# Four-layer GNN stack: the last layer runs its score products ahead of the attended product of two pairs before, and the value product ahead of the new pair's first turn

## What is computed

```python
h = jnp.maximum(_layernorm(x, axis=-1), 0.0)
q = (h @ Wq + bq).reshape(b, n, H, HD); k = ...; v = ...
scores = jnp.einsum('bqhd,bkhd->bhqk', q, k) / jnp.sqrt(jnp.float32(HD))
scores = scores + (1.0 - adj)[None, None, :, :] * -1000000000.0
attn = jax.nn.softmax(scores, axis=-1)
out = jnp.einsum('bhqk,bkhd->bqhd', attn, v).reshape(b, n, d)
x = x + out @ Wo + bo
```

## Time and profile before

| | us |
|---|---|
| median of 3 runs (715.76 to 717.35) | 716.94 |
| the profiled execution, whole | 716.58 |
| its span, first to last instruction | 714.8 |
| PE busy in the span | 692.3 (97%) |
| DVE busy | 627.9 (88%) |
| ACT busy | 555.9 (78%) |
| POOL busy | 462.1 (65%) |

### The profile page before, as it was taken

One profiled execution on the slowest core, in us unless ns is written; L12 is line 12 of the kernel. 1 busy time (PEld: TensorE's weight loads), 2 busy tenths in 40 slices (PEclk: granted clock), 3 DMA queues, 4 the chain that ended last, 5 costly groups with the idle time before them and its releaser, 6 DMA issues.

```text
span 714.8 us, 22548 instructions
## 1 busy us (share of the span) xinstructions
PE 692.3 (97%) x6938; PEld 652.9 (91%) x6938; DVE 627.9 (88%) x2618; ACT 555.9 (78%) x1892; POOL 462.1 (65%) x585
## 2 busy tenths in 40 slices
PE   5999999999999999999998999999999999999996
PEld 5999999999888888889997999999999999999994
DVE  5899888987799999699998999998889998899876
ACT  3665656565689999876665998889888988898895
POOL 2445454554587788588884776776677666766662
DMA  8222310000000000000000000000000000000001
GB/s 246 83 82 89 89 43 0 0 0 2 0 1 2 1 2 1 2 1 0 0 0 1 17 33 17 30 29 30 15 30 29 30 15 30 30 29 16 32 32 45
DMA packets 21710, 20.30 MB, mean 28 GB/s; under 512 B 2449, under 2 KB 21649, under 8 KB 21649
## 3 DMA queue, kind: packets, MB, share of 16 engines
q1 hardware_dynamic: 19456, 18.16, 8.0%
q10 hardware_dynamic: 2192, 1.44, 0.7%
HBM read 11.21 MB, written 8.39 MB: 27 GB/s over the span
## 4 chain that ended last, share of the span: by engine, by line
PE 89%; DVE 3%; ACT 3%; issue 2%; POOL 1%; DMA 1%; POOLq 0%; ACTq 0%; DVEq 0%
PE bank L397 43%; PE bank L1276 8%; PE bank L387 7%; PE bank L166 5%; PE bank L1262 5%; PE bank L1286 4%; PE bank L480 4%; PE bank L837 3%; PE bank L427 3%; PE bank L377 3%; PE bank L461 1%; PE bank L875 1%; PE bank L850 1%; ACT prob L1372 1%; DMA wk<-in_L_gnn_Wk_dram 1%
## 5 line engine op out<-in xcount | busy, mean ns | idle before, releaser
L1372 ACT ACTIVATE prob<-wide,small 128x128 f32<-128x128 f32 x504 | 195.5, 395 | 2.1 <-DVE small L1484 2.1
L1447 POOL TENSOR_TENSOR prob<-prob,small 128x512 f32<-128x512 f32 x127 | 132.3, 1043 | 100.1 <-DVE small L1498 98.1
L1484 DVE CUSTOM_DVE_ANT_0 wide<-bank,mbias 128x128 f32<-128x128 f32 x512 | 115.3, 286 | 0.1
L1372 ACT ACTIVATION_READ_ACCUMULATOR prob<-wide,small 128x1 f32 x504 | 97.2, 193 | 0.0
L155 POOL TENSOR_TENSOR rstd<-vare,mhalf 128x2 f32<-128x2 f32 x104 | 73.3, 704 | 20.5 <-DVE vare L144 20.2
L1276 PE MATMUL bank<-ident,prob 128*128 128x128 f32 x512 | 72.2, 273 | 3.8 <-POOL prob L1447 3.5
L636 POOL TENSOR_TENSOR rnorm<-norm,mhalf 128x2 f32<-128x2 f32 x32 | 22.3, 696 | 81.3 <-ACT relsq L577 81.3
L129 DVE BATCH_NORM_STATS2 stats<-xs 128x6 f32<-128x256 f32 (+1 forms) x176 | 65.6, 415 | 5.9 <-DMA xs<-in_x_dram 5.0
L239 POOL TENSOR_SCALAR xn<-xs,nmean,rstd 128x256 f32<-128x256 f32 x120 | 65.3, 554 | 5.5 <-POOL rstd L155 5.5
L1392 ACT COPY probT<-bank 128x512 f32<-128x512 f32 x96 | 52.3, 580 | 18.7 <-PE bank L1276 18.7
L1276 PEld LDWEIGHTS bank<-ident,prob 128*128 128x128 f32 x512 | 58.3, 140 | 5.5 <-POOL prob L1447 4.8
(11 more groups left out here) (168 smaller groups left out, 1933.1 us busy)
## 6 DMA issues: line engine op xcount, KB each, us to landing
out_dram<-xs SPq DMA_DIRECT2D x31, 256.0 KB, 2.1
xs<-in_x_dram SPq DMA_DIRECT2D x29, 256.0 KB, 2.7
xs<-in_x_dram ACTq DMA_DIRECT2D x1, 512.0 KB, 7.8
xs<-in_x_dram ACTq DMA_DIRECT2D x1, 256.0 KB, 4.3
wq<-in_L_gnn_Wq_dram SPq DMA_DIRECT2D x1, 256.0 KB, 3.9
wk<-in_L_gnn_Wk_dram ACTq DMA_DIRECT2D x1, 256.0 KB, 5.2
wv<-in_L_gnn_Wv_dram SPq DMA_DIRECT2D x1, 256.0 KB, 5.8
w<-in_L_gnn_W_dram SPq DMA_DIRECT2D x1, 256.0 KB, 7.4
```

The source lines that it names most:

```text
L1372: ins = nc.scalar.activation(prob[:, r, i, :], wide[:, r, i, :], ACT.Exp, bias=nmax[r][:, i:i + 1], scale=-1.0, accum_out=rsum[r][:, i:i + 1])
L1447: nc.gpsimd.tensor_tensor(prob[:, r, :, :], prob[:, r, :, :], rinv[r].unsqueeze(2).to_broadcast([128, QUAD, N]), ALU.mult).then_inc(prob_r ...
L1484: nc.vector.tensor_tensor_reduce(out=wide[:, r, i, :], in0=SS[r][:, i * N:(i + 1) * N], in1=mbias[:, :], scale=-1.0, scalar=3e38, op0=ALU. ...
```

## The change

Nothing is added or removed; all instructions and waits stay, and their places change. On TensorE `scores(p)` goes ahead of `attend(p-2)`, and `project_v(p+1)` goes ahead of `turn_prob(p,0)`. On ScalarE `copy_o(p-2)` goes behind `exponentials(p-1,3)`. On VectorE `low_o(p-2)` goes behind `mask_max(p,0)` and `inverse(p-1,3)`, and `inverse(p,2)` behind `copy_v`.

```diff
@@ TensorE, period
+                    scores(p)
                     if has(p, 2):
                         attend(p - 2, (v + 2) % 4)
-                    scores(p)
...
-                    turn_prob(p, 0)
                     if has(p, 0, LAST):
                         project_v(p + 1)
+                    turn_prob(p, 0)
@@ ScalarE, period
-                    if has(p, 2):
-                        copy_o(p - 2)
                     if has(p, 1):
                         exponentials(p - 1, 3)
+                    if has(p, 2):
+                        copy_o(p - 2)
                     exponentials(p, 0)
@@ VectorE, period
-                    if p > 1:
-                        low_o(p - 2)
                     mask_max(p, 0)
                     if p > 0:
                         inverse(p - 1, 3)
+                    if p > 1:
+                        low_o(p - 2)
...
                     copy_k(p + 1)
+                    copy_v(p + 1)
                     inverse(p, 2)
-                    copy_v(p + 1)
```

More of the change, by code:

```diff
@@ L1402, in period @@
                     relu_high(p + 1, TQ1 if isinstance(p, int) and p == 0 else TQ)
+                    if has(p, 1):
+                        exponentials(p - 1, 3)
                     if has(p, 2):
                         copy_o(p - 2)
-                    if has(p, 1):
-                        exponentials(p - 1, 3)
                     exponentials(p, 0)
```

## The result

The changed kernel takes 728.19 us (median of 4, 727.71 to 728.62) where the kernel before takes 716.35 in the same comparison (715.47 to 717.35): 11.8 us more, a ratio of 1.0165 with a 95% interval of 1.0147 to 1.0182. The forecast was 730.7 us, with 726.5 to 734.5 around it. The executions of one kernel come in two sets, with a mean granted clock of 1.000 and of 0.997 to 0.998, and the second takes 0.5 to 1.4 us longer; all four of the changed kernel are in the first, and in most of the experiments the median is taken over both.

A forecast was written before the change was run, and what follows sets the result against it. TensorE, 97% busy, was taken as the bound, its output product made to wait by the later `copy_o`: 29 x 0.50 = 14.5 us, less 0.35 at the start, on 716.58 gives 730.7 us, range 726.5 to 734.5.

The forecast's parts named there:

- What bounds the kernel: TensorE, 97% busy, almost never waits in the 29 full periods; the block whose input is ready latest decides.
- The chain: From the end of `turn_prob(p-1,1)` through ScalarE's copies and exponentials, `copy_o` and `low_o` to the output product, at 577.44.
- S: The moment at which TensorE takes up what follows `turn_prob(p-1,1)`; times in a period are counted from it.
- the other kind of period: Periods in which ScalarE starts 0.11 instead of 0.17 us behind S, so the output product's lateness is 0.36 us.
- The mean lateness: Output product on TensorE starts late by 0.42 or 0.36 us, 0.39 in the mean, in each of 29 periods.
- The longer block: Output product on TensorE, started on an emptied array, takes 1.53 instead of 1.42 us, 0.11 more a period.
- The value product on TensorE: Moving it ahead of `turn_prob(p,0)` costs 0 a period, with 0 to 0.09 us as bounds.
- Start and end: Waits of 1.03 and 0.23 us in periods 0 and 1 filled, together -0.35 us; last period 0.
- VectorE's late copies: `copy_v` may make the scores 0.1 or 0.2 us late, at no cost, since the output product waits 0.39 anyway.
- The rival of a second wait: VectorE's list makes the k product or scores late by 0.1 to 0.3 us a period: 734 to 739; chance 0.10.
- The rival of a saved drain: Transposes and scores on TensorE follow without the 0.20 us change of tiles, chain in time: 710.4 us; chance 0.03.
- The rival of GpSimd's lock on `low_o`: GpSimd's multiply `divide(p-1,3)` holds VectorE's `low_o` up, 20 us more: about 751 us; chance 0.04.

The follow-up runs named there:

- the runs with three, four and five exponentials: Changed kernel with `copy_o` behind three, four (the changed kernel itself) or five exponentials: 718.61, 728.19 and 740.30 us.
- The run with three: Changed kernel with `copy_o` behind three of the four exponentials and `low_o` between `mask_max(p,0)` and `inverse(p-1,3)`: 718.61 us, ratio 1.0032.
- the kernel with two: Changed kernel with `copy_o` behind two of the four exponentials and `low_o` between `mask_max(p,0)` and `inverse(p-1,3)`: 719.73 us, ratio 1.0041.

## Why the prediction was right

- **What bounds the kernel** held: the 29 full periods carried +12.95 of the change, and the block whose input is ready latest, the output product, is the one that waits.
- **The chain** held link by link, in S: the copy at 0.18 (0.17 was read from the rows of before), the first exponential at 1.15 (1.15), `copy_o` at 2.69 (2.70), `low_o` at 3.30 (3.33), its end at 3.99 (4.01), the output product at 4.04 (4.07). In the other kind of period the product comes at 403.04 - 399.07 = 3.97 (4.01). The mean lateness is 0.355 where 0.39 was summed; the runs with three, four and five exponentials show its slope.
- **The longer block** of a product that had to wait held: 1.53 for 1.42, taken from the block behind a change of tiles. The run with three adds that 0.10 is paid even with no wait in sight, when the weights come just in time.
- **The value product on TensorE** was taken at 0 with 0 to +0.09; it is -0.02, outside that bound.
- With these two the sum is 29 x (0.355 + 0.11 - 0.02) = 12.9 instead of 14.5, so 1.6 too high: 1.0 from the lateness and 0.6 from the value product.
- **Start and end**: -0.44 for -0.35, and -0.15 for 0. Of the two waits that were to be gone, the 0.23 is; the 1.03 came back as 0.99 one group later. With these 0.24 and the 0.46 of chance ahead of the first scores the whole is accounted for: the profiled executions differ by 11.9 where +14.15 was forecast.
- **VectorE's late copies**: said to be hidden, and shown so by the changed kernel with L144 moved. The scores were expected 0.1 or 0.2 late in such periods, under the longer wait; they are not late at all. The rival of a second wait did not come in the changed kernel; its mechanism is real, and came in the kernel with two, at 0.22 a time.
- **The rival of a saved drain** fell: with the scores straight behind the transposes they start at 590.63, and the last transposes' block 0.53 ahead, as the attended product's did (572.84 to 573.37). **The rival of GpSimd's lock on `low_o`** fell by the rows of `low_o` and of the multiply; that the multiply would lie over `low_o` was right. The Trainium skill (SBUF — State Buffer, Who interferes with whom) says that a VectorE instruction with two inputs in SBUF contends with a GpSimd instruction that reads SBUF, and that one with at most one does not. The trace agrees in both: L144, with two, is held, `low_o`, with one in PSUM, is not.

## What to carry to other kernels

When a producer and its consumer sit on different in-order engines, an operation moved behind others delays its consumer by the whole group that now stands ahead of it; add up the chain from the last common event (here the end of a group of transposes) and compare it with the time at which the consumer would start. An edit that moves a producer later on the busy engine may leave the other engines' lists nothing to repair: the attended product went 1.1 us later where the slack was 1.07 us, and with the best place of `copy_o` that was tried the weights still came just in time, not early. Parts of such a change are best timed apart: here one of them gained 0.1% and was hidden under the loss of the rest. And gains of a microsecond are best compared between executions at the same granted clock.

## What the runs showed of the hardware that was not expected

A product whose weights arrive just in time shows no wait in any view and is still 0.10 us longer over its 12 matmuls (1.52 against 1.42). And a VectorE operation of two columns, 0.15 us long, can last as long as a 1.04 us GpSimd multiply. In the changed kernel VectorE's and GpSimd's timelines have

```profile
587.72 0.39 DVE L143 SCALAR_TENSOR_TENSOR nmean<-mv 128x2 f32<-128x2 f32 x1
588.03 0.15 DVE L144 SCALAR_TENSOR_TENSOR vare<-mv 128x2 f32<-128x2 f32 x1
```

```profile
586.78 1.31 POOL L1442 TENSOR_TENSOR xs<-xs,rows 128x512 f32<-128x512 f32 x1
588.05 1.04 POOL L1447 TENSOR_TENSOR prob<-prob,small 128x512 f32<-128x512 f32 x1
```

where L144 is short; at 407.54 against 407.55, above, it is long. It was long in 5 to 18 of 29 periods in the kernels that kept its place, but for one with 1, and in none where it was moved to a place in which GpSimd was idle.

That the two start almost together is no accident. L143, just ahead of L144, takes 0.15 us where GpSimd is idle and 0.39 here, and it ends 14 to 26 ns behind GpSimd's bias (L1442; here both end at about 588.1), in all full periods of the kernels that kept its place. So it is held until the bias ends, and then L144 and the next multiply start within 25 ns of each other. Which of them comes first in the rows doesn't decide whether L144 is held: in the changed kernel it is long when it starts 23 ns ahead and short when it starts 1 ns behind. What does decide stays open.
